# Divide-and-conquer merges with third-order root updates, and the diffusion steps as a Horner polynomial

## The reference, cut to what matters

```python
# layer 0: eight Euler steps
h = einsum('bnd,ed->bne', x, fc_in_w) + fc_in_b
alph = sigmoid(alpha_train)[:, None]
w_eff = w * clip(d, 0, 1) @ w.T
for _ in range(8):
    ax = einsum('nm,bmd->bnd', adj, h)
    h = h + (1/8) * (alph * 0.5 * (ax - h) + h @ w_eff - h + x)
# layer 2: the eigenvectors of a normalised Laplacian
deg = sum(A, axis=0) + sum(A, axis=1) - diagonal(A)
L_norm = deg**-0.5 * (diag(deg) - A) * deg**-0.5
_, U = eigh(L_norm)
```

## Time and profile before

| what | us |
|---|---|
| median of 3 runs | 4371.05 (4370.43 to 4371.77) |
| the profiled execution | 4372.59 |
| its span, first to last instruction | 4369.5 |
| PE busy, share of the span | 2968.4 (68%) |
| DVE busy | 3368.4 (77%) |
| ACT busy | 930.0 (21%) |
| POOL busy | 1213.4 (28%) |

### The profile page before, as it was taken

The page is one execution under the profiler, slowest core; times in us unless marked ns, Lnnn a source line. Parts: engine busy times, 40 slices in busy tenths (PEclk is TensorE's granted clock), DMA queues, the critical chain, the costliest instruction groups (busy, mean ns, idle before and its releaser), DMA issues. The chain is left out here.

```text
span 4369.5 us, 81639 instructions
## 1 busy us (share of the span) xinstructions
PE 2968.4 (68%) x21390; PEld 2151.6 (49%) x21390; DVE 3368.4 (77%) x19528; ACT 930.0 (21%) x3812; POOL 1213.4 (28%) x5213
## 2 busy tenths in 40 slices
PE   4787877777766665655346754668888864759694
PEld 3666666666655454444224432334444444647572
DVE  6888888888888888888687888889699738961553
ACT  1221222222233333333111110111111102321201
POOL 2545455555555555555200110000000000000000
PEclk6555555555555555555568877888999967879777
DMA  1000000000000000000110000000000000000001
GB/s 59 2 2 2 2 2 2 2 2 2 2 1 2 1 2 1 1 1 1 44 39 1 1 0 0 0 0 1 0 1 0 1 0 1 0 0 0 0 1 39
DMA packets 22431, 24.06 MB, mean 6 GB/s; under 512 B 2192, under 2 KB 20624, under 8 KB 21520
## 3 DMA queue, kind: packets, MB, share of 16 engines
q1 hardware_dynamic: 22032, 19.47, 1.4%
HBM read 15.28 MB, written 4.19 MB: 4 GB/s over the span
## 5 line engine op out<-in xcount | busy, mean ns | idle before, releaser
L302 PE MATMUL h_sums<-h_P,ones 128*128 128x60 f32 (+3 forms) x1020 | 315.3, 404 | 244.5 <-DVE h_P L488 165.9
L725 PE MATMUL d_acc<-d_h,U 128*128 128x512 f32 x1024 | 474.2, 607 | 0.0
L310 PE MATMUL h_axp<-h_XV,ident 128*128 128x64 f32 x1018 | 337.4, 435 | 182.9 <-POOL h_XV L354 182.9
L283 PE MATMUL h_sums<-h_parts,ones 128*128 128x19 f32 (+2 forms) x1020 | 315.3, 399 | 186.9 <-DVE h_parts L441 165.2
L787 POOL TENSOR_TENSOR m_c_mid<-m_c_m,m_halves 128x4 f32<-128x4 f32 x90 | 90.6, 1007 | 1217.6 <-DVE m_c_m L976 1217.6
L302 PEld LDWEIGHTS h_sums<-h_P,ones 128*128 128x128 f32 x1020 | 254.9, 310 | 305.2 <-issue 305.2
L291 PE MATMUL h_axp<-h_XV,x 128*128 128x4 bf16 x11514 | 388.5, 169 | 16.8 <-DVE h_CX L452 15.5
L283 PEld LDWEIGHTS h_sums<-h_parts,ones 128*128 128x128 f32 x1020 | 256.5, 312 | 272.7 <-DVE h_parts L441 232.9
L310 PEld LDWEIGHTS h_axp<-h_XV,ident 128*128 128x128 f32 x1018 | 254.7, 311 | 265.8 <-DVE h_y L526 216.8
L340 POOL TENSOR_TENSOR h_root<-urow,h_halves 128x1 f32<-128x1 f32 x510 | 277.1, 543 | 382.7 <-DVE urow L493 382.7
L291 PEld LDWEIGHTS h_axp<-h_XV,x 128*128 128x128 bf16 x11514 | 362.4, 105 | 34.0 <-DVE h_CX L452 24.9
(11 more groups left out here) (499 smaller groups left out, 7389.1 us busy)
## 6 DMA issues: line engine op xcount, KB each, us to landing
cut<-in_c_cut SPq DMA_DIRECT2D x1, 4608.0 KB, 13.7
x<-in_x SPq DMA_DIRECT2D x16, 256.0 KB, 5.3
out<-x SPq DMA_DIRECT2D x16, 256.0 KB, 3.7
adj<-in_adj SPq DMA_DIRECT2D x1, 1024.0 KB, 5.2
below<-in_c_below SPq DMA_DIRECT2D x1, 1024.0 KB, 7.6
neps<-in_c_neps SPq DMA_DIRECT2D x1, 1024.0 KB, 8.9
UT<-in_c_ramp SPq DMA_DIRECT2D x1, 1024.0 KB, 10.7
same<-in_c_same SPq DMA_DIRECT2D x1, 448.0 KB, 10.3
```

The source lines that it names most:

```text
L283: nc.tensor.matmul(PS1[:, lo:hi], m.ones[:], parts[:, lo:hi], start=True, stop=True).then_inc(sums_ready, 1)
L302: nc.tensor.matmul(PS2[:, :, T1 * c0:], m.ones[:], P2[:, :, c0:, :].rearrange("p i c t -> p i (c t)"), start=True, stop=True).then_inc(pv_ ...
L310: nc.tensor.matmul(sides(PSE), m.ident[:, r:r + 1].broadcast_to([P, P]), sides(XV[:, cr, 0:2 * RIGHT]), start=True, stop=True).then_inc(ro ...
L725: nc.tensor.matmul(self.acc[:], m.mixT[:, c, r * P:(r + 1) * P], src[:, :, c, :], start=(c == 0), stop=False, skip_group_check=True)
```

## The change

- Root updates are unrolled, with their number and kind per size. Each takes a third moment of the pole sum and models the nearest pole and the one beyond the gap, either by the root of a quadratic (POOL's power, DVE waits) or by a series. The loop of ten goes. The starting value comes from such a quadratic too.
- Where size is up to 128, DVE instructions per chunk become one instruction over all chunks with a broadcast operand; some instructions are reordered, and some landings are waited for later.
- At the end of a level the hand-over between DVE and PE is per chunk: four increments of `sT_ready`, `sT_copied`, `product_ready`.
- The eight Euler steps are a polynomial: h8 = sum over k of M^k x G_k, with M the mixing matrix. Horner's rule needs per step one product with `G[k]` of the turned x (turned once) and one with `mixT`; the accumulator is doubled. Units are dealt to levels by a cost and a budget.
- The G_k are grown in `build_laplacian` on PE and ACT; the bias needs the vectors M^k 1, which `read_tridiagonal` makes on PE and ACT, where POOL also makes `mixT`. `rho` is made by PE there. The load of `cut` and those of `x` are issued at the start of `read_tridiagonal`; `prepare_diffusion` goes.
- `alpha_train` is loaded as four columns instead of a broadcast row, `fc_in_b` as a column, and a table `c_cut_col` is added.

```diff
+CUBIC_ROOT, CUBIC, QUADRATIC = range(3)
+UPDATES = {2: (0, 0, 1), 4: (0, 0, 1, 1), 8: (0, 0, 1, 1), 16: (0, 0, 1, 1, 1), 32: (0, 0, 1, 1, 1, 2),
+           64: (0, 0, 0, 1, 1, 1, 2), 128: (0, 0, 0, 1, 1, 1, 2), 256: (0, 0, 0, 1, 1, 1, 2), 512: (0, 0, 0, 1, 1, 1, 2)}
```

An update after, in `merge_levels` (what stands for the ten of before; `part` cuts to W columns, `K` is a 128x4 column set):

```diff
+                for kind in UPDATES[size]:
+                    do(minus_x("x"))
+                    gx_done = do.send(v.tensor_tensor(K("gx"), K("G"), K("x"), ALU.subtract))
+                    do(v.reciprocal(part(work), part(work)))
+                    for c in range(C):
+                        t = v.tensor_tensor_reduce(scr[:, c, 0:W], work[:, c, 0:W], z2[:, c, 0:W], 1.0, k("sg", c), ALU.mult, ALU.add,
+                                                   k("F", c))
+                    F_done = do.send(t)
+                    wx_done = do.send(v.reciprocal(K("wx"), K("gx")))
+                    do.reach(F_done)
+                    for c in range(C):
+                        t = v.tensor_tensor_reduce(pen[:, c, 0:W], scr[:, c, 0:W], work[:, c, 0:W], k("x", c), 0.0, ALU.mult, ALU.add,
+                                                   k("a1", c))
+                    a1_done = do.send(t)
...
+                    if kind != QUADRATIC:
+                        for c in range(C):
+                            t = v.tensor_tensor_reduce(scr[:, c, 0:W], pen[:, c, 0:W], work[:, c, 0:W], k("x", c), 0.0, ALU.mult,
+                                                       ALU.add, k("a2", c))
+                        a2_done = do.send(t)
...
+                    v.tensor_tensor(K("m2"), K("lo"), K("hi"), ALU.mult).then_inc(root_in, 1)
...
+                    if kind == CUBIC_ROOT:
+                        v.tensor_scalar(K("F4"), K("F"), -4.0, None, ALU.mult)
+                        do(v.tensor_tensor(K("t2"), K("b"), K("b"), ALU.mult))
+                        do(v.tensor_tensor(K("a2"), K("a2"), K("t3"), ALU.add))
+                        do(v.tensor_tensor(K("a2"), K("a2"), K("F4"), ALU.mult))
+                        do(v.tensor_tensor(K("a2"), K("a2"), K("t2"), ALU.add))
+                        v.tensor_scalar(K("disc"), K("a2"), 0.0, None, ALU.max).then_inc(root_in, 1)
+                        roots += 1
+                        dve.wait_ge(root_out, roots)
+                        do(v.tensor_tensor(K("b"), K("b"), K("root"), ALU.add))
```

The level's end, on PE and DVE:

```diff
-                t.then_inc(sT_ready, 1)
-                pe.wait_ge(sT_copied, l + 1)
+                    t.then_inc(sT_ready, 1)
                 for j in range(C):
                     g = j // w * w
+                    pe.wait_ge(sT_copied, l * C + g + w)
...
-                t.then_inc(product_ready, 1)
+                    t.then_inc(product_ready, 1)
...
+                for c in range(C):
+                    dve.wait_ge(sT_ready, l * C + c + 1)
+                    v.tensor_copy(sk[:, c, 0:V], ps[:, c, 0:V]).then_inc(sT_copied, 1)
+                for c in range(C):
+                    dve.wait_ge(product_ready, l * C + (c // (V // P) + 1) * (V // P))
```

The diffusion beside the levels:

```diff
+    COST = {T_STEPS + 1: 0.7, T_STEPS: 1.1}
+    BUDGET = (28, 34, 36, 42, 50, 66, 92, 140, 10000)
...
+            cost = self.COST[k] if k in self.COST else 5.3
+            if spent + cost > self.BUDGET[level]:
+                level, spent = level + 1, 0.0
...
+                for j in range(GROUP):
+                    i = nc.tensor.matmul(acc[:, j, :], self.xT[:, r, j, :], m.G[:, k, :], start=(j == 0),
+                                         stop=(k == T_STEPS), skip_group_check=True)
...
+                if k < T_STEPS:
+                    for c in range(C):
+                        if r == 0 and c == C - 1:
+                            pe.wait_ge(self.taken, n)
+                        i = nc.tensor.matmul(acc, m.mixT[:, c, r * P:(r + 1) * P], src[:, :, c, :], start=False,
+                                             stop=(c == C - 1), skip_group_check=True)
```

Growing the polynomial, on PE in `build_laplacian` (`FB` is 129; ACT copies `pp` back to `poly` after each step; steps 0 and 1 stand ahead of the row matmul, steps 2 to 7 behind it):

```diff
+            def grow(t):
+                pe.wait_ge(poly_taken, t + 2)
+                now, last = poly[:, t % 2], (new if t < T_STEPS - 1 else new_last)
+                for q in range((t + 1) // 3 + 1):
...
+                    i = nc.tensor.matmul(span(a, hi), m.ident[:], now[:, a - 1:hi, :], start=True, stop=False, skip_group_check=True)
+                    if q == 0:
+                        nc.tensor.matmul(pp[:, 0, 0:FB], m.ident[:], last[:], start=False, stop=False, skip_group_check=True)
+                    if lo <= t:
+                        b = min(t, hi)
+                        i = nc.tensor.matmul(span(lo, b), W[:], now[:, lo:b + 1, :], start=False, stop=True, skip_group_check=True)
+                i.then_inc(poly_ready, 1)
```

`rho` and the vectors M^k 1, on PE in `read_tridiagonal`:

```diff
+            for l, size in enumerate(LEVELS):
+                if size <= P:
+                    t = nc.tensor.matmul(rhop[:, l, :], m.same[:, l, :], vals[:, l, :], start=True, stop=True)
+                else:
+                    w = size // P
+                    for c in range(C):
+                        g = c // w * w
+                        for j in range(g, g + w):
+                            t = nc.tensor.matmul(rhop[:, l, c:c + 1], m.ones[:], vals[:, l, j:j + 1], start=(j == g),
+                                                 stop=(j == g + w - 1))
+            t.then_inc(rows_ready, 1)
+            pe.wait_ge(alpha_ready, 4)
+            for k in range(T_STEPS):
+                if k:
+                    pe.wait_ge(u_ready, k)
+                for r in range(C):
+                    for c in range(C):
+                        t = nc.tensor.matmul(ups[:, r:r + 1], m.mixT[:, c, r * P:(r + 1) * P], u[:, c, k:k + 1],
+                                             start=(c == 0), stop=(c == C - 1))
+                t.then_inc(ups_ready, 1)
```

More of the change, by code:

```diff
@@ L679, in _ @@
+            dve.wait_ge(rows_ready, 3)
+            do(v.tensor_copy(m.rho[:], rhop[:]))
+            dve.wait_ge(cut_loaded, 16)
+            for l in range(len(LEVELS)):
+                t = v.tensor_tensor(m.urow[:, l, :], m.cut[:, l, 1, :], sgn[:], ALU.mult)
             do(t)
-            for c in range(C):
-                t = v.tensor_tensor(m.mixT[:, c, :], m.mixT[:, c, :], m.arow[:], ALU.mult)
+            for l in range(len(LEVELS)):
+                t = v.tensor_tensor(m.urow[:, l, :], m.urow[:, l, :], m.cut[:, l, 0, :], ALU.add)
@@ new lines, in __init__ @@
+        self.acc = ctx.enter_context(nc.psum_tensor("d_acc", [P, 2, GROUP, F], F32))
+        self.units = [(g, k, r) for g in range(B // GROUP) for k in range(T_STEPS + 1, -1, -1) for r in range(C)]
+        self.share, spent, level = [[] for _ in LEVELS], 0.0, 0
+        for n, (g, k, r) in enumerate(self.units):
+            cost = self.COST[k] if k in self.COST else 5.3
+            if spent + cost > self.BUDGET[level]:
+                level, spent = level + 1, 0.0
+            self.share[level].append(n)
+            spent += cost
@@ L863, in _, with minus_x @@
                 R = lambda c: m.rho[:, l, c:c + 1]
+                wide = lambda t: t.unsqueeze(2).broadcast_to([P, C, W])
+                every = lambda t: t.unsqueeze(1).broadcast_to([P, C, O])
+                cut = lambda t: t[:, 0:C * W].rearrange("p (c j) -> p c j", c=C)
+                part = lambda t: t[:, :, 0:W]
+                def minus_x(x):
+                    if W < P:
+                        return v.tensor_tensor(part(work), part(dist), wide(K(x)), ALU.subtract)
+                    for c in range(C):
+                        t = v.tensor_scalar(work[:, c, 0:W], dist[:, c, 0:W], col[x][:, c:c + 1], None, ALU.subtract)
+                    return t
@@ L907, in _ @@
                 do(t)
[L908 to L910 removed]
+                v.tensor_scalar(K("last"), K("t"), BIG / 2, None, ALU.is_gt)
+                if W < P:
+                    do(v.tensor_tensor(part(work), part(work), wide(K("t")), ALU.is_equal))
+                else:
+                    for c in range(C):
+                        t = v.tensor_scalar(work[:, c, 0:W], work[:, c, 0:W], k("t", c), None, ALU.is_equal)
+                    do(t)
@@ new lines, in _ @@
+                do(minus_x("half"))
+                v.scalar_tensor_tensor(K("hi"), K("last"), 1.0, K("half"), ALU.add, ALU.mult)
+                v.scalar_tensor_tensor(K("G"), K("last"), BIG, K("gap"), ALU.mult, ALU.max)
+                do(v.reciprocal(part(work), part(work)))
+                for c in range(C):
+                    t = v.tensor_tensor_reduce(scr[:, c, 0:W], work[:, c, 0:W], z2[:, c, 0:W], 1.0, 1.0, ALU.mult, ALU.add,
+                                               k("f", c))
@@ new lines, in _ @@
+                v.tensor_tensor(part(dist), part(dist), part(pen), ALU.add)
+                dve.wait_ge(root_out, roots)
+                do(v.tensor_tensor(K("den"), K("b"), K("root"), ALU.add))
+                do(v.tensor_scalar(K("den"), K("den"), SMALL, None, ALU.max))
+                do(v.reciprocal(K("den"), K("den")))
```

(10 more changed lines are left out.)

600 lines of the change are left out of this document (328 added, 272 removed).

## The result

| what | before | after |
|---|---|---|
| median of 4 runs, same chip | 4370.74 | 4162.12 (4161.79 to 4168.32) |
| profiled execution, its span | 4372.59, 4369.5 | 4161.79, 4159.6 |

The ratio is 0.9526, 95% interval 0.9509 to 0.9542: faster by 208.6 us. The forecast was 4178 us. Between the two profiled executions lie 209.9 us of span.

What follows compares the result with a forecast made beforehand. DVE's instruction list was taken to bound the merge levels. Savings of 168, 20, 26 and 19 us less losses of 24 and 16 gave -193 from 4372.6: 4179.6, as a median 4178 us, range 4110 to 4220.

Steps and rivals of the forecast that it cites:

- Updates, 168 us: Merges' root updates: fewer, dearer unrolled updates take 634 us instead of 802, saving 168 us.
- rival (b): Root updates: per-partition operands are free in multiply-reduces, 35 us less, 4143 us; chance 0.15.
- Heads, 20: Starts of merge levels: fewer per-chunk instructions, mostly up to size 64, save 20 us.
- The stall, 19: End of level 7 (size 256): DVE's wait for ACT's square root goes if diffusion is early enough, saving 19 us.
- (c): Clock rises late in the narrow levels or in the polynomial: 4219 us; chance 0.15.
- (d): Horner units run at half clock in all merges, slower than before: 4447 us; chance 0.02.
- (e): Stall at size 256 stays, its units being budgeted to the same level: 4197 us; chance 0.05.
- Level ends, 26: Ends of merge levels: merged tail operations and chunk-wise hand-over save 26 us.
- Laplacian block, 24: Before the tridiagonalisation: growing the polynomial on PE makes the block end at 73.7 against 50.4, 24 us lost.
- `read_tridiagonal`, 16: Preparation before the merges: PE's rho and eight rounds outlast DVE, merges begin near 2225 instead of 2209.6, 16 us lost.
- The clock of the chain: Eight rounds in `read_tridiagonal`: one-column matmuls taken at half clock, as the tridiagonalisation ran at 0.50 for 2087 us.
- rival (a): Preparation: one-column chain of rounds runs at full clock, saving 36 us, 4142 us; chance 0.15.

Runs made afterwards that it cites:

- old ends' run: Changed kernel with the chunk-wise hand-over at each merge level's end undone (one semaphore each for transposes, copies, products): 4182.25 us.
- run with the fill: Changed kernel plus three useless matmuls of 128 moving columns per step of the tridiagonalisation: 4456.94 us.
- run with one round: Changed kernel with the chain of eight rounds in `read_tridiagonal` cut to one, leaving out higher powers of the mixing matrix: 4121.0 us.
- wide columns: Changed kernel with each matmul of the eight rounds moving its one column 128 times over, same result: 4144.55 us.

## Why the prediction held

The forecast's span was 193 us shorter than before, the measured one 210. Of the 17 us between them 10.5 lie in the level ends, 8.1 behind the merges and 2.4 in the front; heads, preparation and tridiagonalisation take 4 back. Point by point:

**Updates, 168 us: 167.6.** The table has each level 0.2 to 1.9 us above my sum, 639.6 in all against 634. The updates of before are above my sum by as much, 807.2 against 802, so the difference came out closer than its two terms. The prices of landed and passing instructions carried over to code that wasn't in the trace, since DVE's only long wait in an update is the one for POOL: from L1147 to L1150 it is 1.29 us at size 2, which is my 1.01 of POOL and 0.28 of handing over. A per-partition operand does cost a multiply-reduce 0.06 us: 0.14 from start to start at size 2, where one without it takes 0.08. That refutes rival (b).

**Heads, 20: 17.7. The stall, 19: 19.1.** I had 0.1 to 0.3 us too much saved in each head up to size 64, and 0.5 at 128, where nothing is saved. The diffusion was early enough everywhere, so rivals (c), (d) and (e) fell; and with no diffusion beside levels 1 to 8 the merges took as long, so its cost was nothing indeed. No run puts the old passes beside the new updates, so which part of the change ended the stall, the shorter units or their new distribution, isn't separated.

**Level ends, 26: 36.5.** This is the term I mis-sized. The old ends' run splits it. The hand-over is 20.5 where I had 15.7. Of this difference 3.3 us are the clock of the two wide levels' products, which I had not in the sum and which the changed kernel's profile caught at its best; the run with the fill did not have it. Without them the hand-over is near my price: 2.3 and 2.0 at 256 and 512 where I had 2 and 1.8, and 1.8 to 1.9 where I had 1.7. The tail is 16.0 where I had about 10: I counted only the groups of four that become one, and not the landings that fall away where operations were put in another order. I had nothing above size 64, where it is 4.3.

**Laplacian block, 24: 21.6.** The growth lengthens the stage as expected: some 19.4 us of it are the growth and what follows it, by the run without it. My chain ended at 73.7 instead of 72.0. From 46.3 on the clock was 1.00, as I took it.

**`read_tridiagonal`, 16: 16.8**, but by luck, from two errors that cancel. PE's `rho` starts 14.8 us after the tridiagonalisation instead of 9.2, and the rest, 73.8 us, is 4 less than I had (78 from there to the merges; a round takes 7.25 us, not 7.57). Most of the late start is DVE's: beside POOL's products some of its operations take 2.6 to 4.6 times as long (below).

**The clock of the chain.** It stayed at 0.50: rival (a) is refuted for one moving column. The Trainium skill (TensorE: Matmul & The Clock Gate, "What's actually happening") ties the clock to how busy PE has been recently. If PE's busy share of the trace is taken for that, these runs don't agree with it: 96% busy at 0.50 with one column, 94% busy at 0.92 with 128.

**Behind the merges, not predicted: -8.1.** 5.4 of it is `apply_reflectors`, which nobody changed: 119.4 us before, 114.0 after. It isn't the change's merit: its length goes with the clock it happens to get, as the last section shows. Another 2.3 us lie in the last stretch, in which the result is stored (41.8 us before, 39.5 after); no run shows why.

## What to carry to other kernels

Before moving work into a stage, ask which of its engines ends last and when: eight rounds and a polynomial, put into two stages that close with a barrier, cost 38 us here, and one wait of some 7 us once they lay beside the merges, whose PE has gaps. Where one engine's list alone sets the time and its instructions don't wait, the sum of priced instructions can be good to a per cent, for code that hasn't run yet as well (the updates here); what was rounded instead of counted, the tail, came out 6 us short of 16. When the list gets shorter, find out first what is queued behind the hidden work on each engine (here the norm's square root behind ACT's copies), since that is where the next wait appears.

## What the runs showed of the hardware that I had not expected

**The same passes at both clocks.** With one moving column 32 passes took 6.99 us at 0.50; with 128 columns and the same weights they took 3.84 us at 1.00. With three matmuls of 128 moving and 64 stationary columns per step of 4.7 us, among narrow ones, the clock stayed at 0.50.

**DVE is slow beside POOL.** The timelines of POOL and DVE in `read_tridiagonal` of the changed kernel, where POOL multiplies from 2166.9 to 2175.1:

```profile
2166.86 5.34 POOL L727 TENSOR_TENSOR U<-adjT,t_arow 128x512 f32<-128x512 f32 x4 [11.54 <-ACT t_arow L715]
2167.17 1.23 DVE L759 TENSOR_SCALAR t_drow<-t_drow,t_s 128x512 f32<-128x512 f32 x1
2168.33 1.48 DVE L760 TENSOR_SCALAR t_aoff<-t_aoff,t_s 128x512 f32<-128x512 f32 x1
2169.85 1.23 DVE L762 CUSTOM_DVE_ANT_0 t_scr<-t_aoff,ident 128x128 f32<-128x128 f32 x1
```

The first two took 0.48 each before, and a multiply-reduce of this size 0.29. Each of these three ends 0.15 to 0.29 us after one of POOL's products (1.26 to 1.45 us each). The Trainium skill (SBUF — State Buffer, "🔬 SBUF: two separate sides") says that the two share a pair of ports, which a DVE instruction in a two-port mode or with two SBUF inputs needs, and that whichever of them starts first holds it to its end; these rows agree. I had put POOL's products "under PE's rho part" at no cost. They lie ahead of it, beside DVE, and by these rows they delayed it by some 4 us. No run moved them away, so this is a reading of rows and not a test.

**One stage's length goes with the clock it meets.** `apply_reflectors` is the same code in all kernels. Its window after, and in the run with one round:

```profile
3290.10:3404.10 114.00, 74.22 (x254) 44.09 (x254) 41.14 (x118) 0.63 (x1) 0.00 (x0) 0.73 0.00 0
```

```profile
3241.60:3362.90 121.30, 82.58 (x254) 49.84 (x254) 41.26 (x118) 0.63 (x1) 0.00 (x0) 0.66 0.00 0
```

Over the profiled runs it was 113 to 115 us at a mean clock of 0.72 to 0.76, 117 to 118 at 0.70 to 0.71, and 119 to 121 at 0.66 to 0.69. DVE's work is the same to 0.15 us, and PE's, in the two windows shown, 8.4 us longer at the lower clock. This is as large as several of the effects studied, so they were read from the stage that they lie in. The products of the two widest merges vary in the same way, by up to 2 us each. Executions of one kernel lie up to 12 us apart, too (4138 and 4150 with wide columns); whether by these same stages the single profiles don't tell.
